# Splitting weight pieces two per pair, with five places for raw pieces

## The chip, the cores and the metric

The kernel runs on one core of one Trainium2 chip. The metric is the device time of one execution in microseconds; the median of three runs of the kernel before is 1560.1 us (1558.79 to 1561.29). The engines are named PE (TensorE, the matrix engine), DVE (VectorE), ACT (ScalarE), POOL (GpSimd) and SP (SyncE, which here only issues DMA transfers).

## The reference: what is computed

Two layers over 2048 tokens of width 512. Each layer first gates its input with a bidirectional recurrence along time (`cond`), then applies a mixture of experts and adds the result to its input:

```
x = x + ffn0(cond0(x, f, f))   # 8 experts of inner width 256, top 2, one shared expert, RMS norm
x = x + ffn1(cond1(x, f, f))   # 32 experts of inner width 352, top 6, two shared halves
```

In the second layer, for each token t and each of its six experts e with softmax weight g(t, e):

```
h = silu(x[t] @ w1[e]) * (x[t] @ w3[e])
y[t] += g(t, e) * (h @ w2[e])
y[t] += (silu(x[t] @ sw1) * (x[t] @ sw3)) @ sw2     # shared, for every token
```

All matrices are float32. The weights of the 32 routed experts are 32 x 128 x 4352 numbers of 4 bytes as the kernel packs them, and each is read once.

## The kernel before: how the work is laid out and ordered

**Float32 by two halves.** A float32 operand is multiplied as a sum of two float16 values, high and low. A product takes three matmuls: high by high, high by low, low by high. So every weight piece that arrives raw from memory has to be split: ACT scales and rounds it into the high half `Whi` (function `w_hi_`, L1289), then DVE makes the low half as the raw value minus the high one (`w_lo`, L1719 for the wide part and L1722 for a strip of 64 columns). Some earlier pieces are split by POOL instead.

**Pieces.** The weights are cut into 163 pieces (`PIECES`): 0 to 26 belong to the first layer, 27 to 34 to the shared halves of the second, 35 on to its routed experts, four pieces of 128 x 1088 numbers (544 KB) for each expert. Pieces 51 to 54 are expert 4, 55 to 58 expert 5, and so on to piece 162, the last of expert 31. Ten pieces (`AHEAD`) land in unused parts of the weight tiles. All others pass through a ring of two places, `ST`: SP's `w_load` (L1021) of a piece waits until the low half of the piece two before it in the ring is made. `spare` (L824) says which block must be done before a piece's final place in `Whi` and `Wlo` may be overwritten: six experts have places at a time.

**Order.** Every engine runs its part of one list of stages, produced by the generator `stages` (L136). Engines are in order: an instruction that waits holds back all that stand behind it on its engine. `loads(n, upto)` puts up to n loads into the list, of pieces below `upto`, as long as the ring of two has room; `splits(n)` puts in n splits; `weights(n, upto)` does n times loads, one split, loads.

**The second layer.** First the shared halves (32 blocks) are computed while the rows are gated, stored and given their logits. Then the table of places is made: `r_place` and `hot` on DVE with `hot_pe` on PE, and `table1`, which gives the list of rows for each block of 128. POOL gathers the rows of a block by that table (L1118). The gather needs the gate weights `Wd` stored in memory by SP (`r_wts`, L1018).

The routed part is 128 blocks, four to an expert, done as 64 pairs. A pair has three tiles `f_gu` (PE L1988 and L1994: gate and up products, transposed, with both blocks of the pair side by side), for each of which ACT takes a tanh, DVE multiplies, and `f_split` splits the result (ACT L1343, DVE L1766). Then come two `down` (PE L2059), one for each block; ACT evicts the result (L1365) and POOL adds it to the output rows by an indirect accumulating DMA (L1136). A pair's `down` stand in the list within the next pair: the first after the next pair's first tile, the second after its third. Rows of coming blocks are transposed for the tiles either on PE with a copy on ACT (`turn`, L1917 and L1300) or by a DMA transpose issued by SP (`x_turn`, L1010): `by_pe` chooses PE for the first twelve blocks and for every second one afterwards, so pairs 0 to 4 turn both blocks of the next pair on PE, later ones one.

`pair_weights(p)` (L569) is called twice in each pair: after the first `down`, and after the third tile, before the second `down`. It calls `weights`: nothing in pairs 0 and 1, two pieces in each call in pairs 2 to 5, one in each call from pair 6 on. Its limit `ready` keeps loads and splits to pieces whose places are free by then; it rises by four pieces every second pair.

The tiles `FD` and `FN` (L676) belong to the recurrence and to the sum of the first layer's results, `XR` (L686) to the gating of rows. None of them is used in the routed part. `FH`, `FU` and `FS`, which the routed part does use, are in `RT`.

Of the kernel before, what the change touches and what calls it, by code (L numbers as in the profile page):

```python
# [5 lines left out]
P = 128  # L6
T = 2048
D = 512
NT = T // P
ROWS = T + 512  # L10
CAP = 512
F32 = mybir.dt.float32
# [89 lines left out]
def pieces():  # L102
    out = []
    for e in (8, 0, 1, 2, 3, 4, 5, 6, 7):
        for c in range(3):
            out.append((0, e, c * 1024, 1024, e * 3072 + c * 1024, "pool" if 3 <= len(out) < 15 or len(out) % 2 else "dve"))
    for m, e in enumerate([32, 33] + list(range(32))):
        for c in range(4):
            pool = 2 <= m < SLOTS1
            out.append((1, e, c * 1088, 1088, place1(e) + c * (1152 if e < 32 else 1088), "pool" if pool else "dve"))  # L110
    return out


PIECES = pieces()
# [5 lines left out]
AHEAD = (17, 18, 19, 20, 27, 28, 29, 30, 33, 34)  # L120
AHEAD_AT = (18432, 21504, 0, 24576, 3072)
RING = [k for k in range(len(PIECES)) if k not in AHEAD]


def low_count(k):
# [10 lines left out]
def stages():  # L136

    done = dict(load=0, hi=0, lo=0)

    def loads(n, upto):  # L140

        for _ in range(n):
            k = RING[done["load"]] if done["load"] < len(RING) else len(PIECES)
            if k < upto and done["load"] < sum(j < done["lo"] for j in RING) + 2:
                yield "w_load", k
                done["load"] += 1

    def splits(n, low=True):
        for _ in range(n):
            if done["hi"] in AHEAD or done["hi"] in RING[:done["load"]]:  # L150
                yield "w_hi", done["hi"]
                done["hi"] += 1
                if low:
                    yield from low_half()
# [6 lines left out]
    def weights(n, upto):  # L161
        for _ in range(n):
            yield from loads(2, upto)
            yield from splits(1)
            yield from loads(2, upto)
# [309 lines left out]
    for s in range(18):  # L475
        f = NT + s
# [53 lines left out]
        yield from loads(2, 51)  # L530

    yield "r_place", 3
    yield "r_wts", 7
    yield from shared(29, "gu_pe")
    yield from shared(28, "h_turn")
# [32 lines left out]

    def pair_weights(p):  # L569

        if p >= 2:
            ready = 63 + 4 * ((2 * p - 6) // 4) if p >= 3 else 59
            yield from weights(2 if p < 6 else 1, min(ready, len(PIECES)))

    def tile_in(t, what):

# [51 lines left out]
def build(nc, xtok, fT, cst, svec, cond, rout, gatew, W0, W1, Y1):  # L628
    with ExitStack() as ctx:
        ctx.enter_context(nc.allow_low_precision(reason="sums of at most 16 ones are exact in float16"))  # L630

        def sb(name, shape, dt=F32):
            return ctx.enter_context(nc.sbuf_tensor(name, shape, dt))

        def sem(name):
            return ctx.enter_context(nc.semaphore(name))
# [31 lines left out]
        Whi = sb("Whi", [P, 9 * 3072], F16)  # L668
        Wlo = sb("Wlo", [P, 9 * 3072], F16)
        ST = [sb(f"ST{i}", [P, 1088]) for i in range(2)]  # L670
# [2 lines left out]
        EK = sb("wkEK", [P, 512])  # L673
        EU = [sb(f"wkEU{i}", [P, 512]) for i in range(2)]
        EKV = sb("wkEKV", [P, 512])
        FD = [sb(f"wkFD{i}", [P, 512]) for i in range(2)]  # L676
        FN = [sb(f"wkFN{i}", [P, 512]) for i in range(2)]
        RT = [sb(f"RT{i}", [P, 4, 512]) for i in range(2)]
        HT32 = sb("HT32", [P, 512])
        cnd = HT32[:, :].rearrange("p (b k) -> p b k", b=4)  # L680
# [2 lines left out]
        XSp = [XSall[:, i, :, :] for i in range(4)]  # L683
        XG = [sb(f"XG{i}", [P, D + 32]) for i in range(3)]
        zero, squares = XG[0], XG[2]
        XR = [sb(f"XR{i}", [P, 512])[:, :] for i in range(4)] + [XG[i][:, 0:512] for i in range(2)]  # L686

        X1 = [K[0], K[1], EU[0], EU[1], EK, EKV]
        PK = [[FD[0], FN[0]], [FD[1], FN[1]]]
        WSL = sb("WSL", [P, 8])  # L690
# [39 lines left out]
        gaps = [Wlo[:, e * 4608:e * 4608 + 4608].rearrange("p (r n) -> p r n", r=4)[:, :, 1024:1152] for e in range(4)]  # L730
        AB = [gaps[0:2], gaps[2:4], [W[:, 27136:27648].rearrange("p (r n) -> p r n", r=4) for W in (Whi, Wlo)]]
        idt = OT[:, 0:128]
        XG1 = [XG[i][:, :] for i in range(3)] + [OH[:, 0:D + 32]]


# [12 lines left out]
        d_pick = [sem(f"d_pick{i}") for i in range(2)]  # L748
        d_first = sem("d_first")
        d_w = [sem(f"d_w{i}") for i in range(2)]  # L750
        d_ahead = [sem(f"d_ahead{i}") for i in range(len(AHEAD))]
        d_g = [sem(f"d_g{i}") for i in range(3)]
        d_g1 = [sem(f"d_g1{i}") for i in range(4)]
        d_t = [sem(f"d_t{i}") for i in range(4)]
# [15 lines left out]
        f_part, f_x1, f_tanh, f_gate, f_sq, f_var, f_pow, f_turned, f_ht, f_hi, f_lo, f_lgm, f_lg = (sem(n) for n in (  # L770
            "f_part", "f_x1", "f_tanh", "f_gate", "f_sq", "f_var", "f_pow", "f_turned", "f_ht", "f_hi", "f_lo", "f_lgm", "f_lg"))
# [28 lines left out]
        def low(k):  # L800
            who, count = low_count(k)
            return (w_lov if who == "dve" else w_lop), count
# [11 lines left out]
        def staged(k):  # L814

            l, e, c0, cw, at, who = PIECES[k]
            if k in AHEAD:
                m = AHEAD.index(k)
                to = AHEAD_AT[m // 2]
                return (Whi, Wlo)[m % 2][:, to:to + 2 * cw].bitcast(F32), d_ahead[m], 16  # L820
            m = RING.index(k)
            return ST[m % 2][:, 0:cw], d_w[m % 2], 16 * (m // 2 + 1)

        def spare(k):  # L824

# [22 lines left out]
        def place_of(z):  # L848
# [9 lines left out]
            if z < 71:  # L858
                return XG[2][:, 0:512].bitcast(F16)
            return XG1[(z - 71) % 4][:, 0:512].bitcast(F16)  # L860

# [77 lines left out]
        def _(eng):  # L939
# [35 lines left out]
            def x_load(f):  # L975
# [3 lines left out]
                if f == 4:  # L979
                    eng.wait_ge(d_zero, 16 * 12)  # L980
                S.dma_start(XR[f % 6], xtok[f * P:f * P + P, :]).then_inc(d_x[f % 6], 16)

# [38 lines left out]
            def w_load(k):  # L1021
                l, e, c0, cw, at, who = PIECES[k]
                if k not in AHEAD and k >= 2:
                    eng.wait_ge(*low(RING[RING.index(k) - 2]))
                if k in AHEAD and l == 1:


                    eng.wait_ge(b_down, R0 + {24576: 0, 0: NT, 3072: 2 * NT}[AHEAD_AT[AHEAD.index(k) // 2]])
                at, there, count = staged(k)
                S.dma_start(at, WD[l][e][:, c0:c0 + cw]).then_inc(there, 16)  # L1030
# [25 lines left out]
        def _(eng):  # L1056
# [7 lines left out]
            def k_num_(n):  # L1064
                eng.wait_ge(k_sn, n + 1)
                eng.wait_ge(k_euv, n + 1)
                if n + 1 < 32:

                    eng.wait_ge(k_min, n + 2)
                G.tensor_tensor(FN[n % 2][:, :], FN[n % 2][:, :], EU[n % 2][:, :], ALU.add).then_inc(k_num, 1)  # L1070

# [17 lines left out]
            def gather(n):  # L1089
# [18 lines left out]
                else:  # L1108
# [5 lines left out]
                    if j >= 4:  # L1114
                        x_read(eng, xslot(n - 4))
                        eng.wait_ge(b_wsl, j - 3)
                    to, there = XG1[j % 4], d_g1[j % 4]
                G.indirect_dma_start(  # L1118
# [42 lines left out]
        def _(eng):  # L1161
# [20 lines left out]
            def k_fwd(n):  # L1182
# [4 lines left out]
                eng.wait_ge(k_fd, n + 1)  # L1187
                A.activation(FD[n % 2][:, 0:511], FD[n % 2][:, 0:511], ACT.Copy, scale=gain).then_inc(k_gd, 1)
                eng.wait_ge(k_fn, n + 1)
                A.activation(FN[n % 2][:, 0:511], FN[n % 2][:, 0:511], ACT.Copy, scale=gain).then_inc(k_gn, 1)  # L1190

# [18 lines left out]
            def f_tanh_(f):  # L1210
                if f < NT:
                    eng.wait_ge(d_x[f % 6], 16 * (f // 6 + 1))
                    src = XR[f % 6]
                else:
# [5 lines left out]
                    if f % 6 in (4, 5):  # L1220
                        for z in (S1 - 3, S1 - 2):
                            x_there(eng, z)
                A.activation(XR[f % 6], src, ACT.Tanh, scale=0.5).then_inc(f_tanh, 1)

            def f_sq_(f):
                eng.wait_ge(f_gate, f + 1)
                if f >= 1:
                    eng.wait_ge(f_sq, f)
                A.activation(squares[:, 0:512], XR[f % 6], ACT.Square, accum_out=sm[:, f, 0:1]).then_inc(f_sq, 1)

            def f_hi_(f):
# [10 lines left out]
                if z > S1:  # L1242

                    eng.wait_ge(d_row[(f - 1) % 6], 16 * rows_stored(f - 1))
                    x_there(eng, z - 1)
                A.activation(place_of(z)[:, 0:512], XR[f % 6], ACT.Copy,
                             scale=sm[:, f, 2:3] if l == 0 else XS).then_inc(f_hi, 1)
# [127 lines left out]
        def _(eng):  # L1375
# [49 lines left out]
            def k_fwd(n):  # L1425
                f = FN[n % 2]
                eng.wait_ge(k_min, n + 1)
                V.tensor_tensor_scan(FD[n % 2][:, :], decay(n), EK[:, :], 0.0, ALU.mult, ALU.add).then_inc(k_fd, 1)  # L1428
                eng.wait_ge(k_ekv, n + 1)
# [4 lines left out]
            def k_bwd(n):  # L1434

                f = FN[n % 2]
                dc = decay(n)[:, 0:511]
                eng.wait_ge(k_gd, n + 1)
                V.tensor_tensor_scan(FD[n % 2][:, 510::-1], dc, FD[n % 2][:, 510::-1], FD[n % 2][:, 511:512], ALU.mult,  # L1439
                                     ALU.add).then_inc(k_sd, 1)  # L1440
# [4 lines left out]
            def k_den_(n):  # L1445
                u = EU[n % 2]
                eng.wait_ge(k_eu, n + 1)
                eng.wait_ge(k_sd, n + 1)
                V.scalar_tensor_tensor(out=FD[n % 2][:, :], in0=u[:, :], scalar=E30, in1=FD[n % 2][:, :], op0=ALU.min,  # L1449
                                       op1=ALU.add).then_inc(k_den, 1)  # L1450
# [4 lines left out]
            def k_rec_(n):  # L1455
                eng.wait_ge(k_den, n + 1)
                V.reciprocal(FD[n % 2][:, :], FD[n % 2][:, :]).then_inc(k_rec, 1)  # L1457

            def k_out_(n):
                f = FN[n % 2]  # L1460
                eng.wait_ge(k_num, n + 1)
# [5 lines left out]
            def gate(f):  # L1467
# [4 lines left out]
                if l == 1 and i >= 8:  # L1472
                    eng.wait_ge(d_back[i - 8], 16)
                x = XR[f % 6]
                V.scalar_tensor_tensor(out=x, in0=x, scalar=1.0, in1=RT[b % 2][:, q, :],
# [250 lines left out]
            def weight(n):  # L1726
# [4 lines left out]
                if j >= 8:  # L1731
                    eng.wait_ge(b_outa, NB0 + j - 7)
                V.tensor_copy(WSL[:, n % 8:n % 8 + 1], XG1[j % 4][:, D + e:D + e + 1]).then_inc(b_wsl, 1)

# [396 lines left out]
```

## Time and profile before

| | |
|---|---|
| median of three runs | 1560.1 us (1558.79 to 1561.29) |
| the profiled execution, its own time | 1559.94 us |
| its span in the trace | 1558.1 us |
| PE busy | 1313.3 us, 84% of the span |
| DVE busy | 1084.5 us, 70% |
| ACT busy | 780.9 us, 50% |
| POOL busy | 616.6 us, 40% |
| mean granted PE clock | 0.951 of full |

The span is the time from the first to the last instruction in the profile. "Busy" counts computing instructions. The granted clock is the share of full speed that TensorE was given. A line number such as L1766 is a line of the kernel before. "ST<-W" is a transfer of a raw weight piece into the ring. In the timelines, the bracket behind an instruction gives how long its engine stood idle before it, and what ended the idle time.

### The profile page before, as it was taken

To read this page: it belongs to the slowest core of one execution; us is meant where nothing else is said; L and a number is where in the kernel's file an instruction comes from. 1 tells how busy PE (TensorE), PEld (TensorE's weight loads), DVE (VectorE), ACT (ScalarE), POOL (GpSimd) and SP (SyncE) were. 2 spreads that over 40 slices of the span, in tenths; PEclk is the share of its full clock that TensorE was granted. 3 is DMA by queue.
4 is the path that set the end of the run, shared out by engine and by line. 5 is a ranking of instruction groups with operands and counts; after the bars stand their busy time and mean duration, and the time that the engine had idled before them with its cause. 6 is when DMAs were issued, how large, how long until landed. Compare 5 with 4: busy or idle time off the path is not lost.

```text
span 1558.1 us, 26165 instructions
## 1 busy us (share of the span) xinstructions
PE 1313.3 (84%) x9124; PEld 883.9 (57%) x9124; DVE 1084.5 (70%) x2186; ACT 780.9 (50%) x1451; POOL 616.6 (40%) x478
## 2 busy tenths in 40 slices
PE   0046565599999599999897999999999999999997
PEld 0023352244444366566565677777777777777775
DVE  8999988979898668888655555665565656556332
ACT  4466654645554453441255455555555555555333
POOL 2343443444342343330133444444444444444442
PEclk9988766899999799999999999999999999999999
DMA  3557556677896686541258899989998899899664
GB/s 104 170 162 200 145 117 135 133 194 179 225 247 156 178 225 182 160 132 50 94 147 196 171 212 214 206 202 216 200 214 214 194 222 200 207 226 190 116 117 59
DMA packets 224191, 269.28 MB, mean 173 GB/s; under 512 B 148608, under 2 KB 148736, under 8 KB 223936
## 3 DMA queue, kind: packets, MB, share of 16 engines
q1 hardware_dynamic: 187408, 175.58, 44.5%
q0 software_dynamic: 36656, 92.03, 27.8%
q8 instruction: 76, 1.25, 0.3%
q14 instruction: 51, 0.42, 0.1%
HBM read 167.87 MB, written 70.32 MB: 153 GB/s over the span
## 4 chain that ended last, share of the span: by engine, by line
PE 66%; DVE 22%; issue 5%; DMA 3%; ACT 3%; POOL 0%; SPq 0%; POOLq 0%; ACTq 0%; DVEq 0%
PE psO L2059 21%; PE psG L1988 20%; PE psG L1956 10%; DVE wkFD L1457 5%; PE psH L1988 5%; PE psG L1994 3%; DMA ST<-W 3%; DVE wkFD L1439 2%; PE psX L1917 2%; DVE wkFN L1432 2%; DVE wkFD L1428 2%; DVE Wlo L1719 1%; DVE wkFN L1464 1%; DVE wkFD L1449 1%; ACT Whi L1289 1%
## 5 line engine op out<-in xcount | busy, mean ns | idle before, releaser
L1136 POOL DMA_INDIRECT out<-OB,posb x128 | 221.2, 1728 | 393.1 <-ACT OB L1365 288.9
L1988 PE MATMUL psG<-XSp,Whi 128*128 128x256 f16 x2048 | 342.7, 273 | 2.5 <-ACT XSp L1300 2.5
L1988 PE MATMUL psG<-XSp,Wlo 128*128 128x256 f16 x1024 | 279.6, 273 | 0.0
L1956 PE MATMUL psG<-Whi,XSp 128*128 128x352 f16 (+2 forms) x952 | 258.6, 362 | 9.7 <-issue 8.4
L2059 PE MATMUL psO<-Whi,RT 128*128 128x512 f16 x768 | 253.4, 385 | 14.9 <-DVE RT L1766 14.9
L1719 DVE SCALAR_TENSOR_TENSOR Wlo<-ST,Whi 128x1024 f16<-128x1024 f32 (+1 forms) x116 | 142.2, 1226 | 160.0 <-ACT Whi L1289 154.8
L1988 PEld LDWEIGHTS psG<-XSp,Whi 128*128 128x128 f16 x2048 | 200.4, 98 | 47.9 <-ACT XSp L1300 2.8
L1747 DVE SCALAR_TENSOR_TENSOR RT<-RT,psG 128x256 f32<-128x256 f32 (+1 forms) x154 | 64.6, 419 | 134.5 <-ACT RT L1335 130.7
L1956 PEld LDWEIGHTS psG<-Whi,XSp 128*128 128x128 f16 x952 | 97.6, 103 | 102.0 <-issue 32.5
L1956 PE MATMUL psG<-Wlo,XSp 128*128 128x352 f16 (+2 forms) x476 | 151.6, 363 | 0.0
L1365 ACT ACTIVATE OB<-psO,WSL 128x512 f32<-128x512 f32 x128 | 87.3, 682 | 123.3 <-PE psO L2059 118.4
L2059 PE MATMUL psO<-Wlo,RT 128*128 128x512 f16 x384 | 147.7, 385 | 0.0
L2059 PE MATMUL psO<-Whi,HS 128*128 128x512 f16 (+1 forms) x412 | 140.2, 389 | 0.5 <-DVE OB L1795 0.5
L1289 ACT ACTIVATE Whi<-ST 128x1088 f16<-128x1088 f32 (+1 forms) x116 | 128.1, 1106 | 16.7 <-DMA ST<-W 15.6
L2059 PEld LDWEIGHTS psO<-Whi,RT 128*128 128x128 f16 x768 | 75.9, 99 | 104.2 <-DVE RT L1766 22.5
L1118 POOL DMA_INDIRECT XG<-xrows,posb x96 | 96.3, 1003 | 97.2 <-DVE posb L1649 54.8
L1335 ACT ACTIVATE RT<-psG 128x256 f32<-128x256 f32 (+1 forms) x154 | 58.8, 382 | 113.1 <-PE psG L1988 87.7
L1070 POOL TENSOR_TENSOR wkFN<-wkFN,wkEU 128x512 f32<-128x512 f32 x32 | 40.5, 1266 | 186.7 <-DVE wkEK L1419 175.6
L1457 DVE RECIPROCAL wkFD<-wkFD 128x512 f32<-128x512 f32 x32 | 107.0, 3345 | 0.0
L1988 PEld LDWEIGHTS psG<-XSp,Wlo 128*128 128x128 f16 x1024 | 100.3, 98 | 11.7
L1821 PE MATMUL psX<-C,wkFN 128*128 128x128 f32 x64 | 16.2, 401 | 100.7 <-DVE wkFN L1464 100.7
L1083 POOL TENSOR_TENSOR Wlo<-ST,Whi 128x1024 f16<-128x1024 f32 x33 | 70.2, 2128 | 68.5 <-ACT Whi L1293 68.5
(254 smaller groups left out, 2564.5 us busy)
## 6 DMA issues: line engine op xcount, KB each, us to landing
ST<-W SPq DMA_DIRECT2D x130, 544.0 KB
ST<-W SPq DMA_DIRECT2D x23, 512.0 KB
slots<-OB SPq DMA_DIRECT2D x39, 256.0 KB
wkK<-fT SPq DMA_DIRECT2D x32, 256.0 KB
xrows<-XG SPq DMA_DIRECT2D x20, 256.0 KB, 3.3
y0rows<-x SPq DMA_DIRECT2D x8, 512.0 KB, 5.3
y0rows<-OB POOLq DMA_DIRECT2D x16, 256.0 KB
out<-OB SPq DMA_DIRECT2D x16, 256.0 KB
```

Source lines behind the costliest of these rows:

```text
L1083: op = G.tensor_tensor(Wlo[:, at:at + w], st[:, 0:w], Whi[:, at:at + w], ALU.subtract)
L1118: G.indirect_dma_start(out=to, out_offset=None, in_=X[l][:, :], in_offset=bass.IndirectOffsetOnAxis(ap=idx[l][:, j:j + 1], axis=0)).then_i ...
L1136: G.indirect_dma_start(out=Y1[:, :], out_offset=bass.IndirectOffsetOnAxis(ap=idx[1][:, j:j + 1], axis=0), in_=OB[o % 4][:, :], in_offset=N ...
L1289: op = A.activation(st if who == "pool" else hi, st, ACT.Copy, scale=WS)
L1335: A.activation(FH[p % 2][0:rows, c, :], f_psum(t)[0:rows, 0:256], ACT.Tanh, scale=0.5 * UN).then_inc(b_ftanh, 1)
L1365: A.activation(OB[o % 4][:, :], psO[bank(o)][:, :], ACT.Copy, scale=scale).then_inc(b_outa, 1)
L1457: V.reciprocal(FD[n % 2][:, :], FD[n % 2][:, :]).then_inc(k_rec, 1)
L1719: op = V.scalar_tensor_tensor(out=Wlo[:, at:at + w], in0=st[:, 0:w], scalar=WS, in1=Whi[:, at:at + w], op0=ALU.mult, op1=ALU.subtract)
L1747: V.scalar_tensor_tensor(out=H[0:rows, :], in0=H[0:rows, :], scalar=1.0, in1=ps[0:rows, 0:256], op0=ALU.add, op1=ALU.mult).then_inc(b_fsil, 1)
L1956: op = M.matmul(o, hx[:, x, q * P:q * P + P], w(half_, off + c, nn), start=first, stop=last)
L1988: op = M.matmul(sums(half_ * 256), W[:, to:to + P], x(which, q), start=(q == 0 and which == 0 and W is Whi), stop=(q == 3 and W is Wlo))
L2059: op = M.matmul(psO[bank(o)][:, :], h(x, q), w(half_, off0 + q * 512), start=(q == 0 and x == 0 and half_ is Whi and first), stop=(q == NK ...
```

## The change

In `pair_weights`, pairs 1 on split one piece in each call (two per pair), instead of two in each call in pairs 2 to 5 and one from pair 6 on. The number of places for raw pieces is five from piece 51 on: the two of `ST`, and three in a new tensor `FX`, which also holds what were the tiles FD, FN and XR 0 to 3. A load waits for the low half of the piece five before it; the loads into the three new places wait, the first time, until the rows that used that memory are turned and split (`f_x1`, `f_turned`, `f_lo`). The limit `ready` holds for splits only. The first five loads (pieces 51 to 55) stand in the list behind the last `r_place` and ahead of the last `r_wts`, of the last `hot`s and of `table1`. The semaphores of the AHEAD pieces are used again for the five places, counted on from their first use.

```diff
--- before.py
+++ after.py
@@ -120,6 +120,7 @@
 AHEAD = (17, 18, 19, 20, 27, 28, 29, 30, 33, 34)
 AHEAD_AT = (18432, 21504, 0, 24576, 3072)
 RING = [k for k in range(len(PIECES)) if k not in AHEAD]
+WIDE = RING.index(51)
 
 
 def low_count(k):
@@ -141,7 +142,7 @@
 
         for _ in range(n):
             k = RING[done["load"]] if done["load"] < len(RING) else len(PIECES)
-            if k < upto and done["load"] < sum(j < done["lo"] for j in RING) + 2:
+            if k < upto and done["load"] < sum(j < done["lo"] for j in RING) + (2 if k < 51 else 5):
                 yield "w_load", k
                 done["load"] += 1
 
@@ -530,6 +531,7 @@
         yield from loads(2, 51)
 
     yield "r_place", 3
+    yield from loads(5, 56)
     yield "r_wts", 7
     yield from shared(29, "gu_pe")
     yield from shared(28, "h_turn")
@@ -568,9 +570,11 @@
 
     def pair_weights(p):
 
-        if p >= 2:
+        if p >= 1:
             ready = 63 + 4 * ((2 * p - 6) // 4) if p >= 3 else 59
-            yield from weights(2 if p < 6 else 1, min(ready, len(PIECES)))
+            if done["hi"] < min(ready, len(PIECES)):
+                yield from splits(1)
+            yield from loads(5, len(PIECES))
 
     def tile_in(t, what):
 
@@ -673,8 +677,9 @@
         EK = sb("wkEK", [P, 512])
         EU = [sb(f"wkEU{i}", [P, 512]) for i in range(2)]
         EKV = sb("wkEKV", [P, 512])
-        FD = [sb(f"wkFD{i}", [P, 512]) for i in range(2)]
-        FN = [sb(f"wkFN{i}", [P, 512]) for i in range(2)]
+        FX = sb("FX", [P, 8 * 512])
+        FD = [FX[:, i * 512:i * 512 + 512] for i in range(2)]
+        FN = [FX[:, i * 512 + 1024:i * 512 + 1536] for i in range(2)]
         RT = [sb(f"RT{i}", [P, 4, 512]) for i in range(2)]
         HT32 = sb("HT32", [P, 512])
         cnd = HT32[:, :].rearrange("p (b k) -> p b k", b=4)
@@ -683,7 +688,7 @@
         XSp = [XSall[:, i, :, :] for i in range(4)]
         XG = [sb(f"XG{i}", [P, D + 32]) for i in range(3)]
         zero, squares = XG[0], XG[2]
-        XR = [sb(f"XR{i}", [P, 512])[:, :] for i in range(4)] + [XG[i][:, 0:512] for i in range(2)]
+        XR = [FX[:, i * 512 + 2048:i * 512 + 2560] for i in range(4)] + [XG[i][:, 0:512] for i in range(2)]
 
         X1 = [K[0], K[1], EU[0], EU[1], EK, EKV]
         PK = [[FD[0], FN[0]], [FD[1], FN[1]]]
@@ -730,6 +735,7 @@
         gaps = [Wlo[:, e * 4608:e * 4608 + 4608].rearrange("p (r n) -> p r n", r=4)[:, :, 1024:1152] for e in range(4)]
         AB = [gaps[0:2], gaps[2:4], [W[:, 27136:27648].rearrange("p (r n) -> p r n", r=4) for W in (Whi, Wlo)]]
         idt = OT[:, 0:128]
+        STW = [ST[WIDE % 2], ST[1 - WIDE % 2]] + [FX[:, i * 1088:i * 1088 + 1088] for i in range(3)]
         XG1 = [XG[i][:, :] for i in range(3)] + [OH[:, 0:D + 32]]
 
 
@@ -748,7 +754,7 @@
         d_pick = [sem(f"d_pick{i}") for i in range(2)]
         d_first = sem("d_first")
         d_w = [sem(f"d_w{i}") for i in range(2)]
-        d_ahead = [sem(f"d_ahead{i}") for i in range(len(AHEAD))]
+        d_staged = [sem(f"d_staged{i}") for i in range(len(AHEAD))]
         d_g = [sem(f"d_g{i}") for i in range(3)]
         d_g1 = [sem(f"d_g1{i}") for i in range(4)]
         d_t = [sem(f"d_t{i}") for i in range(4)]
@@ -817,9 +823,12 @@
             if k in AHEAD:
                 m = AHEAD.index(k)
                 to = AHEAD_AT[m // 2]
-                return (Whi, Wlo)[m % 2][:, to:to + 2 * cw].bitcast(F32), d_ahead[m], 16
+                return (Whi, Wlo)[m % 2][:, to:to + 2 * cw].bitcast(F32), d_staged[m], 16
             m = RING.index(k)
-            return ST[m % 2][:, 0:cw], d_w[m % 2], 16 * (m // 2 + 1)
+            if m < WIDE:
+                return ST[m % 2][:, 0:cw], d_w[m % 2], 16 * (m // 2 + 1)
+            i = (m - WIDE) % 5
+            return STW[i][:, 0:cw], d_staged[i], 16 * ((m - WIDE) // 5 + 2)
 
         def spare(k):
 
@@ -1021,7 +1030,16 @@
             def w_load(k):
                 l, e, c0, cw, at, who = PIECES[k]
                 if k not in AHEAD and k >= 2:
-                    eng.wait_ge(*low(RING[RING.index(k) - 2]))
+                    m = RING.index(k)
+                    if m < WIDE + 2:
+                        eng.wait_ge(*low(RING[m - 2]))
+                    elif m < WIDE + 5:
+
+                        eng.wait_ge(f_x1, NT)
+                        eng.wait_ge(f_turned, 2 * NT)
+                        eng.wait_ge(f_lo, 2 * NT)
+                    else:
+                        eng.wait_ge(*low(RING[m - 5]))
                 if k in AHEAD and l == 1:
```

## Rows read from the trace of the kernel before

**Rows 1.** The page, part 2: busy tenths of PE and DMA engines, 40 slices.

```profile
PE   0046565599999599999897999999999999999997
...
DMA  3557556677896686541258899989998899899664
```

**Rows 2.** Windows: length, busy of PE, PEld, DVE, ACT, POOL, clock, DMA share, GB/s.

```profile
789.79:869.22 79.43, 66.99 (x497) 47.09 (x495) 43.13 (x98) 42.04 (x69) 27.96 (x20) 0.91 0.77 177
869.22:1438.90 569.68, 568.77 (x4514) 421.43 (x4513) 337.86 (x815) 315.40 (x576) 264.21 (x192) 1.00 0.92 208
```

**Rows 3.** Timeline of PE, 800 to 870: start, length, instruction, idle before, releaser.

```profile
806.92 0.60 PE L2059 MATMUL psO<-Whi,RT 128*128 128x512 f16 x1 [2.30 <-DVE RT L1766]
...
824.95 0.61 PE L2059 MATMUL psO<-Whi,RT 128*128 128x512 f16 x1 [3.97 <-DVE RT L1766]
...
841.94 0.39 PE L2059 MATMUL psO<-Whi,RT 128*128 128x512 f16 x1 [1.72 <-DVE RT L1766]
...
858.32 0.61 PE L2059 MATMUL psO<-Whi,RT 128*128 128x512 f16 x1 [4.45 <-DVE RT L1766]
```

**Rows 4.** Chain of waits, 798 to 805: start, length, what.

```profile
798.77 5.11 DMA ST<-W
...
803.90 1.12 ACT Whi L1289
```

**Rows 5.** Waits of POOL and SP, 795 to 905: total us, times, longest.

```profile
POOL out L1136 <- DMA out<-OB,posb: 12.3, 4, 3.7
...
SPq L1030 <- DVE Whi L1722: 81.1, 16, 31.2
```

**Rows 6.** Chain of waits, stamps in the routed part.

```profile
789.79 2.62 PE psG L1988 x24
...
866.83 0.45 PE psX L1917 x8
...
869.22 2.62 PE psG L1988 x24
...
1000.49 2.62 PE psH L1988 x24
...
1057.79 1.94 PE psO L2059 x9
1059.73 2.62 PE psH L1988 x24
1062.35 2.03 PE psO L2059 x9
```

**Rows 7.** Window around the second of the four waits.

```profile
824.00:832.00 8.00, 7.05 (x30) 3.85 (x31) 3.01 (x9) 2.88 (x4) 5.38 (x4) 0.57 0.65 172
```

**Rows 8.** Chain of waits at pair 15, and PE's timeline behind it.

```profile
965.69 6.34 DMA ST<-W
...
979.34 0.39 PE L2059 MATMUL psO<-Whi,RT 128*128 128x512 f16 x1 [0.91 <-DVE RT L1766]
```

**Rows 9.** DMA issues, one line, a window, timelines of SP and POOL.

```profile
Whi<-W SPq DMA_DIRECT2D x3, 544.0 KB, 5.8
...
L1457 DVE RECIPROCAL wkFD<-wkFD x32: 3332/3346/3347, 17.0 to 496.9; 128x512 f32<-128x512 f32 x32
...
760.00:772.00 12.00, 9.51 (x75) 6.67 (x76) 2.85 (x9) 2.52 (x4) 4.25 (x5) 1.00 0.83 275
...
742.04 0.38 SPq L1018 DMA_DIRECT2D xrows<-Wd  x1
...
758.26 0.96 POOL L1118 DMA_INDIRECT XG<-xrows,posb  x1 [54.81 <-DVE posb L1649]
```

**Rows 10.** L1010, the DMA transposes: one issue, all landings, PE's wait.

```profile
1002.97 8.44 SPq L1010 DMA_TRANSPOSE XSp<-XG  x2
...
DMA to landing us min/median/max: 2.8/4.5/9.3
...
PEld psG L1988 <- DMA XSp<-XG: 0.3, 1, 0.3
```

## The prediction, made before the changed kernel was run

> **What bounds the kernel now.** I read the page's slices first [rows 1]: behind slice 14 PE falls below nine tenths only in slice 20 (8), the passage into the routed part, whose pairs run from 767 us on, and in slice 22 (7), 818 to 857 us, inside it. The table by stretches says how much that is: from 869.22 to 1438.90 PE is busy 568.77 of 569.68 us at a clock of 1.00, while 789.79 to 869.22 has 66.99 busy of 79.43 at 0.91 [rows 2]. So the routed part is bound by TensorE, and what a change of the weight supply can give back is what PE loses to waiting, plus what it then loses to the lower clock.
>
> PE's own timeline names the waits [rows 3]: 2.30, 3.97, 1.72 and 4.45 us, 12.44 in all, each before the first matmul of a `down` (L2059) and each released by DVE L1766, the second half of `f_split`. That step doesn't need the weights just split. The chain of waits shows why it is late [rows 4]: a transfer "DMA ST<-W" of 5.11 us, and right behind its landing ACT L1289, then DVE L1719. ACT and DVE work in order, so a split whose raw piece has not landed stands ahead of the eviction, the cast and the subtraction that `down` waits for. With four splits per pair and two places a load can start only once the piece two before it is split, so from the third piece on each split waits for a whole transfer; SP waited 81.1 us in 16 such waits [rows 5].
>
> The pairs are read from stamps in the chain [rows 6]. Pair 2 begins at 789.79, pair 7 at 869.22. With two splits per pair, 1000.49 and 1059.73 are the same tile five pairs apart: 59.24 us, 11.85 a pair. In it the first `down` of a pair takes 2.03 for its nine matmuls, the second 1.94: 0.09 late behind the split at the end of the pair before.
>
> **The change part by part.** *Two splits per pair from pair 1 on.* The same pieces are split by the same instructions (ACT 1.12 us [rows 4]), but one in each of the two calls of `pair_weights`, as in the steady part. An ideal for pairs 2 to 6 follows from rows. Pairs 0 to 4 turn both blocks of the next pair on PE; one such turn is 0.45 us (L1917) [rows 6]. Pairs 2, 3 and 4 are then 11.85 + 0.45 = 12.30, pairs 5 and 6 11.85: 36.90 + 23.70 = 60.60 us. They take 79.43. The difference is 18.83: 12.44 of idle PE and 6.39 of slower matmuls. The granted clock was 0.57 between 824 and 832, around the wait that ended at 824.95 [rows 7], and 1.00 in the stretch behind 869 without such waits: the lower of the two levels, 1.2 GHz for 2.4, comes after PE has stood still. Without the waits both go.
> The Trainium skill ("TensorE: Matmul & The Clock Gate", Part 1) has the same shape: the slow clock is the resting state of the array. By it the 6.39 us have no cause of their own and go with the waits. Another cause of the dips, were there one, would leave the 6.39 us in: 1546.9 by the sum below, and that is part of the first rival.
> Pair 1 gets two splits that it did not have. They cost it between nothing and their whole length on ACT, 2 by 1.12; I take what they cost a steady pair, 0.1, since the two places in the order are the same. The queue is now behind that of before (piece 63 next at pair 7, was 67), so the last piece is split two pairs later, in pair 56: twice 0.1 more. Expert 4 (pieces 51 to 54) is ready in pair 2 and needed in pair 8, each later one likewise six pairs ahead, some 70 us.
>
> *Five places.* In steady flow each split releases one load, as before, but the load is for the piece five on, so it has some 2 pairs (24 us) before its split, against 5.8 us median for a transfer of that size [rows 9]. Before, the limit `ready` made loads come in bursts: at pair 15 one asked for at 965.69 took 6.34 us, and PE lost 0.91 behind it [rows 8]. That is the only idle PE between 869 and 1439 [rows 2], and it goes: -0.91, or 0 if something else takes its place.
> The places are FD, FN and XR made into one tensor. Moving tiles costs nothing that rows show: the reciprocals on the two FD tiles take 3332 to 3347 ns [rows 9]. 15 ns by 32 is 0.5 us either way; I take 0 and keep this end.
>
> *Five loads ahead of the table.* SP issues them before the Wd store at 742.04, and their waits (row tiles turned and split) are fulfilled by then. Issuing costs SP 5 by 0.38 = 1.9 us (the Wd store's own 0.38 taken for each) [rows 9]. SP waits there for DVE to make Wd, which hides it; without that cover it is 1.9. The transfers are 5 by 544 KB, 2.79 MB. At the 275 GB/s that 760 to 772 shows this is 10 us, one after the other at 5.8 us it is 29. Started near 732, ten us ahead of the store, they have landed between 742 and 761. Behind them comes the Wd store, which the first gather needs at 758.26 [rows 9]. So the cost lies between 0 and some 761 + 2 - 758.3 = 4.7 us (2 for the store itself, an estimate from a size an eighth of a piece's). The DMA engines are busy one to two tenths in slices 19 and 20 [rows 1], so I take 0. Below nothing: two loads no longer meet the first gathers, and PE is idle 12.00 - 9.51 = 2.5 us in 760 to 772; that much at most comes back, I take 0, since the gathers were issued before those loads.
> The Trainium skill ("DMA: Bandwidth & Descriptors", Queues, rings and completion order) says that each DMA engine works through the descriptors of one issuer's row in ring order. By it the Wd store has to stand behind all five loads; by the first rate it still lands at about 745, and the sum stays; by the second it costs the 4.7. The same rule makes the third rival below possible.
>
> **Sum**: 1559.94 (profiled execution, span 1558.1) - 18.83 - 0.91 + 0.1 + 0.2 = 1540.5. The median of the runs, 1560.1, is 0.2 from it: 1540.6 us as forecast of the median. Everything downstream is shifted only: the last matmuls and the last scatters come at the same distance.
>
> **Rivals.**
> 1. *A new wait takes the place.* Pairs 1 to 4 have one more turn on PE (0.45 us) with its copy on ACT than the steady pairs, and scatters and gathers start there. If a wait of 1 us per pair stayed in pairs 1 to 6 and held the clock down as before, half of it again, 6 by 1.5 = 9 us come back: 1549.6. For: `f_split` already is 0.09 late in every steady pair [rows 6], so there is no slack. Against: the added copy comes before the tile that ACT waits for anyway. Chance 0.08.
> 2. *The Wd store is held up* by the five loads: +4.7, 1545.3. Against: the idle DMA engines. Chance 0.03.
> 3. *Slower: the transposes miss their pair.* The block transposes (L1010) stand on SP behind the load that waits for the second split. Before, that was so in every other pair, because `ready` kept loads out of the rest; now it is so in every pair from 5 on. In such a pair the transpose is issued 2.5 us after the pair's start (1002.97 against 1000.49), and the next pair starts 9.4 us later (1000.49 + 11.85) [rows 6, 10]. Landings were 2.8 to 9.3 us, median 4.5, and PE waited for one once, 0.3 us [rows 10]. If the newly exposed 24 or so pairs landed 1 us past that, 24 us go: 1564.5. It decides from 0.8 us mean overshoot on. Against: some 25 pairs had this order already, with one wait of 0.3 us seen [rows 10]. Chance 0.04.
> 4. *It does not do what it says:* the early pairs stay late for another reason, for example the scatters, for which POOL waits 12.3 us between 795 and 905 [rows 5]. Near 1560. Against: these waits are POOL's, and ACT's eviction is not shown waiting for them. Chance 0.03.
>
> **How the numbers follow.** The forecast has 0.82. Its own range is 1537.6 (2.5 at the start and 0.5 of tiles come back) to 1544 (pair 1 costs 2.2, the 0.9 stays). The range given is 1537.5 to 1548: with the main case and parts of rivals 1 and 2, some 0.88. A measurement of this kernel tells about 0.2% (3 us) from no change. Faster by over 0.2%: 0.82 + 0.08 + 0.03 = 0.93; same 0.03 (rival 4); slower 0.04 (rival 3).
>
> **What would show it.** Right: PE busy all through 790 to 850 at clock 1.00; no "DMA ST<-W" in the chain after 765; pair 7's first tile at about 850.5; splits at two per pair from about 783 on, the last two pairs later in count, five pairs still at 59.24; five loads between 732 and 742; first gather still at 758. Wrong: an idle entry at L2059 in the early pairs (rival 1), the first gather later than 758.3 with "xrows<-Wd" landing late (2), PEld waits on "DMA XSp<-XG" spread over the routed part and five pairs above 59.3 (3), or pair 7 again at 869 (4).

## The result, and the profile after

The changed kernel takes 1550.5 us (median of 7 runs, 1549.59 to 1564.81); the kernel before 1562.24 (7 runs, the three of its own table among them, 1558.79 to 1564.6). The ratio is 0.9939, 95% interval 0.9912 to 0.9965: faster by 0.6%, half of the forecast 1.25%, and 2.5 us above the upper end of the range. The spread is new: 15 us between its runs, for 6 before. All ratios here and below leave out runs more than 1.5% above the fastest of their kernel, which is one run, of the kernel with two places. The profiled execution is the slowest of the seven, 1564.81 us, with a span of 1563.0; so its losses stand for the bad end of that spread.

The slices, PE and DMA, against [rows 1]: slice 22 now holds a 9, but slices 27 (1016 to 1055 us) and 29 (1094 to 1133 us), which held a 9, have an 8.

```profile
PE   0046675599999599999899999989899999999997
...
DMA  3557546678995686543269999999999989999664
```

Windows of the changed kernel, with the columns of [rows 2]. The first runs from the first tile of pair 2 to the end of the last `down` in pair 6, the second is the stretch of [rows 2].

```profile
789.71:850.23 60.52, 60.52 (x494) 44.99 (x492) 35.38 (x86) 35.65 (x64) 27.43 (x20) 1.00 0.80 170
869.22:1438.90 569.68, 552.72 (x4346) 408.06 (x4344) 326.37 (x783) 303.62 (x554) 254.78 (x187) 0.99 0.98 201
```

The early pairs are what the sum said: 60.52 us, PE busy in all of them, clock at 1.00 (forecast 60.60; before, 79.43). The stretch behind, which had 0.91 us of idle PE, now has 569.68 - 552.72 = 16.96. The waits of the changed kernel between 852 and 1440 (total us, times, longest) say for what:

```profile
POOL out L1154 <- DMA out<-OB,posb: 120.4, 22, 10.4
PEld psG L2006 <- DMA XSp<-XG: 17.1, 9, 4.0
PE psG L2006 <- DMA XSp<-XG: 13.0, 7, 3.5
PEld psH L2006 <- DMA XSp<-XG: 7.3, 3, 3.6
PE psH L2006 <- DMA XSp<-XG: 5.7, 2, 3.1
```

On the weight-load side PE waited 17.1 + 7.3 = 24.4 us in 12 places for DMA transposes; before, 0.3 in one [rows 10]. On the matmul side PE stood still for 18.7 us. The forecast's sum in terms of the span was 1538.7; 1563.0 - 1538.7 = 24.3. The 5.6 us between 18.7 and 24.3 fit slower matmuls: in the second stretch one takes 552.72 / 4346 = 127.2 ns for 568.77 / 4514 = 126.0 before, some 5 us in all, at a granted clock of 0.99 for 1.00. So in this execution the transposes account for the whole difference. The chain of waits shows one of them, at pair 22:

```profile
1031.18 1.02 ACT Whi L1307
...
1033.36 0.23 DVE Whi L1740
...
1033.61 0.33 SPq L1048
...
1034.04 12.44 DMA XSp<-XG
...
1046.53 2.79 PE psH L2006 x24
```

Second split of pair 21 on ACT, its end on DVE, then SP's load (L1048, the old L1030), which waited for it, then the transpose (L1019, the old L1010) behind that load: 12.44 us to landing, and the first tile of the next pair starts with it. No wait for a raw piece (ST<-W, FX<-W) is left in the routed part.

### The profile page after: what moved, and what is told of

It reads as the page before. It is cut to its first block, busy times and chain, and to the rows that moved or that the text cites. A ratio compares the mean times of both kernels' runs of the same rounds, so it can differ in the third digit from the quotient of the medians.

```text
span 1563.0 us, 26168 instructions
## 1 busy us (share of the span) xinstructions
PE 1316.7 (84%) x9124; PEld 884.0 (57%) x9124; DVE 1085.6 (69%) x2186; ACT 779.8 (50%) x1451; POOL 616.0 (39%) x478
## 3 DMA queue, kind: packets, MB, share of 16 engines
q8 instruction: 76, 1.25, 0.3%
## 4 chain that ended last, share of the span: by engine, by line
PE 61%; DVE 22%; DMA 7%; issue 6%; ACT 3%; SPq 0%; POOL 0%; POOLq 0%; ACTq 0%; DVEq 0%
PE psG L2006 19%; PE psO L2077 18%; PE psG L1974 9%; DMA XSp<-XG 6%; DVE FX L1475 5%; PE psH L2006 5%; PE psG L2012 3%; DVE FX L1457 2%; DVE FX L1450 2%; DVE FX L1446 2%; PE psX L1935 2%; DVE FX L1482 1%; DVE FX L1467 1%; DVE FX L1460 1%; DVE H L1793 1%
## 5 line engine op out<-in xcount | busy, mean ns | idle before, releaser
L2077 PE MATMUL psO<-Whi,RT 128*128 128x512 f16 x768 | 249.6, 380 | 1.5 <-DVE RT L1784 1.5
L2006 PEld LDWEIGHTS psG<-XSp,Whi 128*128 128x128 f16 x2048 | 200.6, 98 | 63.0 <-DMA XSp<-XG 17.1
L1737 DVE SCALAR_TENSOR_TENSOR Wlo<-FX,Whi 128x1024 f16<-128x1024 f32 x66 | 80.9, 1226 | 88.6 <-ACT Whi L1307 83.5
L1088 POOL TENSOR_TENSOR FX<-FX,wkEU 128x512 f32<-128x512 f32 x32 | 40.5, 1266 | 185.3 <-DVE wkEK L1437 174.1
L1475 DVE RECIPROCAL FX<-FX 128x512 f32<-128x512 f32 x32 | 107.1, 3346 | 0.0
L1737 DVE SCALAR_TENSOR_TENSOR Wlo<-ST,Whi 128x1024 f16<-128x1024 f32 (+1 forms) x50 | 61.4, 1228 | 61.9 <-ACT Whi L1307 61.8
L1839 PE MATMUL psX<-C,FX 128*128 128x128 f32 x64 | 16.3, 404 | 99.2 <-DVE FX L1482 99.2
```

The lines of the kernel that those rows point to most:

```text
L1737: op = V.scalar_tensor_tensor(out=Wlo[:, at:at + w], in0=st[:, 0:w], scalar=WS, in1=Whi[:, at:at + w], op0=ALU.mult, op1=ALU.subtract)
L2006: op = M.matmul(sums(half_ * 256), W[:, to:to + P], x(which, q), start=(q == 0 and which == 0 and W is Whi), stop=(q == 3 and W is Wlo))
L2077: op = M.matmul(psO[bank(o)][:, :], h(x, q), w(half_, off0 + q * 512), start=(q == 0 and x == 0 and half_ is Whi and first), stop=(q == NK ...
```

## The experiments

Two theories. **A, the order on SP:** in the changed kernel every transpose stands behind a load that waits for the second split. It is issued late, its data stand behind 544 KB in the same queue, and its packets then run among the scatters'. **B, the traffic:** five places and denser loads slow the transposes whatever the order.

**The changed kernel again.** 

> The changed kernel once more, beside the others. In its first trace pairs 2 to 6 took what was forecast, but TensorE waited 24.4 us (weight-load side) for DMA transposes, in 12 places, while its time went from 1549.6 to 1564.8 us between runs. Both theories: about 1550 us median, some 10 us under before, with a spread of several us, and waits on 'DMA XSp<-XG' of 8 to 25 us in the profile.

Measured: 1553.92 us (7 runs, 1543.31 to 1558.15), before 1562.11 (18 runs); ratio 0.9931 (0.9904 to 0.9958). Its profile has waits of 14.1 + 2.1 us on transposes in 7 places. The loss is there again, in other pairs and of another size.

**Loads held by `ready`.**

```diff
-            yield from loads(5, len(PIECES))
+            yield from loads(5, min(ready, len(PIECES)))
```

> The changed kernel with the limit `ready` put back on the loads only: five places, two splits per pair and the five loads ahead stay. The second call of every second pair then issues no load, so the transposes of every second pair go out at once, as before the change. Theory A (a transpose that stands behind a load, which itself waits for the second split, is issued some 2.5 us late in every pair, and meets the scatters and gathers): the waits on transposes fall to under 3 us, the spread goes, 1541 to 1544 us. Rival B (the transposes are slow because of what five places let onto the DMA engines, whatever the order): no better than the changed kernel, about 1550.

Measured: 1541.04 us (1539.45 to 1544.54), ratio 0.987 (0.9849 to 0.9891). No wait on a transpose is left. SP's timeline shows both kinds of pair. The transpose at 1061.38 goes out with no waiting load right ahead of it; the one at 1076.97 stands behind three loads (from 1064.70 on), the last of them waiting for a split.

```profile
1058.60 0.33 SPq L1048 DMA_DIRECT2D ST<-W  x1
1061.38 1.24 SPq L1019 DMA_TRANSPOSE XSp<-XG  x1
1064.70 12.18 SPq L1048 DMA_DIRECT2D FX<-W  x3
1076.97 1.24 SPq L1019 DMA_TRANSPOSE XSp<-XG  x1
```

Five places, the early loads and the number of bytes are as in the changed kernel. What differs is when loads go out, and with it that only every second transpose stands behind one. So five places alone are not the cause. That the loads now come in bursts is a difference too; the kernel after the next one has no bursts.

**Two places.** The kernel before, with one split per call from pair 1 on:

```diff
-        if p >= 2:
+        if p >= 1:
             ready = 63 + 4 * ((2 * p - 6) // 4) if p >= 3 else 59
-            yield from weights(2 if p < 6 else 1, min(ready, len(PIECES)))
+            yield from loads(2, len(PIECES))
+            if done["hi"] < min(ready, len(PIECES)):
+                yield from splits(1)
+            yield from loads(2, len(PIECES))
```

> The kernel before with one part of the change alone: one split per call from pair 1 on, and loads not held by `ready`; two places, the old memory, no loads ahead of the table. A load follows each split, as in the changed kernel. Theory A: the early waits go (the load has about a pair's time), the transposes stand behind a load in every pair, so like the changed kernel, 1547 to 1556. Rival B: without the five places the transposes land in time, 1541 to 1544. If the early gain needs the five loads ahead, a wait for ST<-W shows in pair 1 to 3 instead.

Measured: 1557.65 us (12 runs, 1547.84 to 1571.29), ratio 0.9965 (0.994 to 0.9991). The median (1557.01 without the highest run) is above the range given by A; with that spread I don't read more from it than that the loss is there without the five places. Together with the loads held by `ready`, B falls. Waits and chain of its profile:

```profile
PEld psG L1991 <- DMA XSp<-XG: 11.4, 6, 4.1
...
839.18 12.96 DMA XSp<-XG
```

No wait on ST<-W stands in it: with one split per call, a load has about a pair's time, and two places are enough.

**The load behind the transpose.** The changed kernel, the second call without its load, and the load after the next pair's `x_turn`:

```diff
         yield from turn(n + 2, False)
+        if p >= 2:
+            yield from loads(5, len(PIECES))
...
-        yield from pair_weights(p)
+        yield from pair_weights(p, False)
```

> The changed kernel with the load of the second call moved in the list behind the next pair's x_turn, nothing else: no transpose stands behind a load that waits for the second split, in any pair. Theory A: every transpose is issued about when the pair starts and lands within 4 us; no waits on transposes, 1540 to 1542 us. Rival B: the same traffic, so waits as before, about 1550.

Measured: 1541.81 us (1539.8 to 1545.54), ratio 0.9873 (0.9851 to 0.9896), no wait on a transpose. A transpose of SP's timeline, and the first tile of the pair from the chain: the transpose for the pair after goes out 2.3 us before this pair starts.

```profile
1072.96 1.24 SPq L1022 DMA_TRANSPOSE XSp<-XG  x1
...
1075.28 2.62 PE psG L2009 x24
```

The loads are not held by `ready` here, and nothing but their place behind the transpose differs from the changed kernel. So the order is the cause. What in it? A late issue, a load ahead, or both together? Three kernels part them.

**Late, but nothing ahead.** The order above, and each transpose also waits for the second split:

```diff
             def x_turn(z):
+                if z >= 71:
+                    eng.wait_ge(*low(halved[-1]))
```

`halved[-1]` is the last split that stands in the list before the transpose.

> The order of e3 (load behind the transpose), but each transpose of the routed part also waits for the second split of the pair before, so it is issued as late as in the changed kernel (about 2.2 us after the pair's start) with no load ahead of it. If the lateness alone is what makes the transposes miss: waits on them as in the changed kernel, 1549 to 1556. If the load ahead in the queue is needed: 1541 to 1543.

Measured: 1543.26 us (1540.56 to 1545.47), ratio 0.9887 (0.9867 to 0.9906), no wait on a transpose though it is issued 2.06 us into the pair:

```profile
1077.99 1.42 SPq L1025 DMA_TRANSPOSE XSp<-XG  x1
...
1075.93 2.62 PE psG L2013 x24
```

**Early, but behind a load.** The load is held until the transpose may go, and issued right ahead of it:

```diff
+            def w_load_at(kz):
+                k, z = kz
+                gathered(eng, z)
+                x_free(eng, ring_before(z))
+                w_load(k)
```

In the list `w_load_at` stands right ahead of `x_turn(z)`.

> Five places, but the second load of a pair is held until the next transpose may go and is issued directly ahead of it, without waiting for the last split. The transpose is early (about 0.4 us before the pair's start) and stands behind a load's 544 KB. If standing behind the load is enough to miss: waits as in the changed kernel, 1549 to 1556. If lateness is needed too: packets of the transposes run some 3 us after the issue, end before the pair's scatters, 1541 to 1543.

Measured: 1539.69 us (1539.38 to 1541.41), ratio 0.9865 (0.9846 to 0.9884), no wait. A load and its transpose, and the start of the pair, 1.16 us later (1.9 in the middle case):

```profile
1061.36 0.33 SPq L1056 DMA_DIRECT2D ST<-W  x1
1061.78 1.24 SPq L1027 DMA_TRANSPOSE XSp<-XG  x1
...
1062.94 2.62 PE psG L2020 x24
```

**At the eviction, nothing ahead.**

```diff
             def x_turn(z):
+                if z >= 71:
+                    eng.wait_ge(b_outa, routed_of(z - 4))
```

> The order of e3, but each transpose of the routed part waits for ACT's eviction of the pair's first block, the same event that releases POOL's scatter, some 5.4 us after the pair's start; no load stands ahead of it. The next pair starts 6.4 us later. If what counts is that the transpose's packets run together with a scatter's: landings well above 6.4 us, waits in many pairs, above 1560. If a load ahead is needed: a landing takes the 4.5 us of the others, few waits, 1541 to 1546.

Measured: 1541.53 us (4 runs, 1539.41 to 1542.38), ratio 0.9876 (0.9838 to 0.9914). Issued 5.41 us into the pair, later than in any other kernel, the transposes still land in time, but for two waits of 1.1 us in all:

```profile
1067.78 1.24 SPq L1025 DMA_TRANSPOSE XSp<-XG  x1
...
1062.37 2.62 PE psG L2012 x24
...
PEld psH L2012 <- DMA XSp<-XG: 0.6, 1, 0.6
PEld psG L2012 <- DMA XSp<-XG: 0.5, 1, 0.5
```

Neither lateness alone nor a load ahead alone costs anything. My expectation here assumed that a transpose released with the scatter meets it. It doesn't: its packets come after the scatter's (packet records below).

**Small scatters.** The changed kernel, but POOL's routed scatters write 16 rows of each block's 128; the other rows of the routed result are left out.

```diff
-  ...(ap=idx[1][:, j:j + 1], axis=0), in_=OB[o % 4][:, :], ...
+  ...(ap=idx[1][0:16, j:j + 1], axis=0), in_=OB[o % 4][0:16, :], ...
```

> The changed kernel, whose routed scatters write 16 of 128 rows of each block and leave the others out (the loads, the transposes and their order stay). If the transposes are slow because their small packets run among those of the scatters (and the gathers that these push back): waits on transposes under 1 us in all, 1538 to 1541. If the weight loads are what slows them: waits as in the changed kernel, about 1550.

Measured: 1535.81 us (4 runs, 1535.41 to 1537.04), ratio 0.9836 (0.9814 to 0.9858). Loads and transposes stand as in the changed kernel, load first, 0.42 us apart, and no transpose makes PE wait; POOL's own wait for scatters between 780 and 1540 us is down from 132.2 us in the changed kernel (first line) to 36.6:

```profile
POOL out L1154 <- DMA out<-OB,posb: 132.2, 27, 10.4
...
POOL out L1154 <- DMA out<-OB,posb: 36.6, 24, 2.9
...
1065.02 0.33 SPq L1048 DMA_DIRECT2D FX<-W  x1
1065.44 1.24 SPq L1019 DMA_TRANSPOSE XSp<-XG  x1
```

So the late order does harm only with full scatters beside it (and the gathers that they push). The time is 2.2 us under the range expected and 3.9 under the best of the others; that fits the shorter last scatters, but was not taken apart.

**What the packets show.** The trace keeps the record of every single DMA packet: a transpose is 1024 packets of 256 bytes, a scatter's packets are of 2048 bytes, a gather's and a load's of 4352. The table has the medians of some 50 transposes of each trace, issued between 835 and 1440 us. "Issue" is against the start of the pair, "first" and "last" are the first and the last packet against the issue, "ns" is the mean time of its packets, "scatter" and "gather" are how many packets of these fell between the first and the last, and "slow" counts transposes whose last packet came more than 7.5 us after the issue. Even and odd pairs stand apart where they differ ("only two parts" is the last kernel below).

```
kernel                        issue   first   last    ns   scatter  gather   slow
before, even pairs            +2.5    +2.5    +6.2    36   96       6        3
before, odd pairs             -1.0    +1.2    +2.7    21   2        0        0
changed                       +2.5    +2.6    +6.2    38   108      10       18
two places                    +2.5    +2.7    +6.1    32   108      12       9
loads by ready, even          +2.5    +2.5    +5.9    29   97       4        2
loads by ready, odd           -1.2    +2.1    +3.8    27   1        0        0
load behind transpose, even   -2.3    +1.5    +5.0    29   100      0        0
load behind transpose, odd    -2.3    +2.1    +4.2    30   2        0        0
only two parts, even          -2.3    +1.5    +4.9    31   112      0        0
only two parts, odd           -2.3    +2.1    +3.8    25   2        0        0
late, nothing ahead           +2.1    +1.2    +2.6    21   3        0        0
early, behind a load, even    -1.9    +3.1    +5.8    22   112      0        0
early, behind a load, odd     -1.9    +2.6    +5.4    36   0        0        0
at the eviction               +5.4    +2.0    +4.3    22   0        60       0
changed, 16-row scatters      +2.5    +2.7    +4.4    22   12       26       0
```

A load directly ahead moves the first packet from +1.2 to between +2.5 and +3.1. Alone that is harmless, as 2.1 us of late issue are. Together they put the transposes where a scatter and the gathers behind it run: the 18 slow ones of the changed kernel met 124 scatter and 46 gather packets in the middle case, and there a 256-byte packet takes 60 ns and not 21. At the eviction the transposes are later still and have slipped past the scatter: none met.

Neither kind of packet is enough alone. In the three kernels "load behind transpose", "only two parts" and "early, behind a load", 51 transposes met 80 or more scatter packets and under 10 gather packets; the latest last packet among them is at +7.1. (Of such transposes issued late behind a load, 2 of 11 in the kernel before and 1 of 9 in the changed one are slow, at +7.9 at most.) At the eviction and with 16-row scatters, 89 met 20 or more gather packets and under 20 scatter packets; there the latest is at +5.9. In the changed kernel 25 met 80 or more scatter and 10 or more gather packets, and 16 of them are slow. A transpose that is slow also has more time to meet others, so the counts alone don't say what comes first. The small scatters show that the scatter's packets are needed; no run takes the gathers away.

The Trainium skill ("DMA: Bandwidth & Descriptors", Queues, rings and completion order) has both halves: one issuer's descriptors are consumed in ring order on each engine, and an engine takes turns between the rows that have work, packet by packet. The shift by 1.3 to 1.9 us behind a load agrees with the first. The second agrees in kind; in size it is not enough by itself, since 124 scatter packets at 0.25 us, their mean in the changed kernel, over 16 engines are 1.9 us (worked out from this case's packet records), and the last packet of the 18 slow transposes comes at +9.8, 3.6 us later than the middle one, which met 108.

**Only two parts.** The kernel before, one split per call from pair 1, and the second load behind the transpose. Two places, nothing ahead of the table, the old memory:

```diff
-    def pair_weights(p):
+    def pair_weights(p, load=True):
-        if p >= 2:
+        if p >= 1:
-            yield from weights(2 if p < 6 else 1, min(ready, len(PIECES)))
+            if p == 1 and load:
+                yield from loads(2, len(PIECES))
+            if done["hi"] < min(ready, len(PIECES)):
+                yield from splits(1)
+            if load:
+                yield from loads(2, len(PIECES))
...
         yield from turn(n + 2, False)
+        if p >= 2:
+            yield from loads(2, len(PIECES))
...
-        yield from pair_weights(p)
+        yield from pair_weights(p, False)
```

> The kernel before with one split per call from pair 1 on, and the second load of a pair behind the next pair's x_turn; two places, no loads ahead of the table, the old memory. If the five places and the early loads are worth nothing here, as the traces of e2 suggest (no wait on ST<-W in it): 1541 to 1543, like e3. If the places matter once the loads are one transpose later: waits on ST<-W and 1545 or more.

Measured: 1540.57 us (1539.04 to 1542.53), ratio 0.9868 (0.9849 to 0.9887). First tile of pair 2 and of pair 7 in its chain, 60.59 us apart:

```profile
788.54 2.62 PE psG L1995 x24
...
849.13 2.62 PE psG L1995 x24
```

This is as good as the best with five places (1539.69, intervals overlap) and beats both the kernel before and the changed one.

## Why the prediction was wrong

**Two splits per pair: right, to 0.1 us.** Pairs 2 to 6 take 60.52 us against 60.60 forecast, at full clock, so the 6.39 us of slower matmuls went with the 12.44 of waits. Six kernels with this step, the full scatters and at most 2 of some 50 transposes over 7.5 us measure 1539.7 to 1543.3, the forecast being 1540.6.

**Five places: the step that failed.** The sum gave them -0.91 for the load burst at pair 15, and that wait is gone. But the other effect of letting loads run past `ready`, a load that waits for a split ahead of every transpose, was put among the rivals with 0.04, and it is what happened: 24.4 us in the profiled execution, about 10 in the median. The reasons given against it were two, and both were weak:

- "Landings were 2.8 to 9.3 us" [rows 10]. The changed kernel's answer of the same kind reads 3.1/4.4/6.7, while its chain shows transposes of 10.4 to 13.7 us. That line speaks only for the transposes whose landing the view can tell, and none of these is in the routed part: asked for 780 to 1540 us alone, it gives no landing in either kernel. The chain and the packets do. In the kernel before, the last packet of a transpose behind a load came at +6.2 us in the middle case and at +8.6 at most, of the 9.4 us that the prediction counted; the median of 4.5 promised 4.9 us of room where there were 3.2.
- "Some 25 pairs had this order already", with one wait of 0.3 us. True, but in the kernel before each such pair was followed by one without a load in front. Slack that exists in every second pair is not slack in a row. Of the 12 waits in the changed kernel, 8 are for transposes issued in even pairs, and 7 of these stood behind such a load before, too. Their surroundings had changed, not their place in the list. Of the 4 in odd pairs, the newly exposed ones (6.3 of the 24.4 us), 3 come right behind a wait: those issued in pairs 7, 27 and 35 follow those of 6, 26 and 34. With `ready` back on the loads, every second pair is free again and no wait is left.

The size in the rival was right for the slowest execution (24 us, 1564.5 against 1564.81 measured) and wrong for the middle one. Its point of decision was a mean of 0.8 us over the 24 newly exposed pairs. The profiled execution has 24.4 / 24 = 1.0, and is indeed slower than the median of before (1562.24); the median execution has some 10 / 24 = 0.4, and the change stays faster. That the 24 us agree is luck: they were worked out as 1 us in each newly exposed pair, and three quarters of the measured waits are in the other pairs.

**Five early loads: right, and worth nothing.** SP issued them at 732.20 to 734.8, and the Wd store and the first gather came when they had before (742.04 and 758.26 in [rows 9]). Timelines of SP and POOL in the changed kernel:

```profile
732.20 0.92 SPq L1048 DMA_DIRECT2D ST<-W  x2
733.23 1.55 SPq L1048 DMA_DIRECT2D FX<-W  x3
741.95 0.38 SPq L1027 DMA_DIRECT2D xrows<-Wd  x1
...
758.18 0.96 POOL L1136 DMA_INDIRECT XG<-xrows,posb  x1 [54.38 <-DVE posb L1667]
```

The bound of 2.5 us below nothing came to 9.59 - 9.51 = 0.08 us of PE:

```profile
760.00:772.00 12.00, 9.59 (x76) 6.74 (x77) 2.85 (x8) 2.44 (x4) 4.16 (x5) 1.00 0.60 182
```

The kernel with two places and no early loads is as fast as those with both, so neither carries any of the gain.

**The other rivals.** No wait at `down` took the place of the old ones (rival 1), Wd was not held up (rival 2), and the early pairs did not stay late (rival 4).

**What stays open.** Why the loss varies by 15 us between executions of one program, and why it comes in clusters of pairs (9 of the 12 waits of the first trace are for transposes issued in pairs 20 to 48, 7 of them in pairs 20 to 35). POOL's waits for its own scatters between 852 and 1440 us rose to 120.4 us from what they were in the kernel before:

```profile
POOL out L1136 <- DMA out<-OB,posb: 70.3, 22, 4.6
```

So a slow transpose may delay the scatter that meets the next one; that is argued, and no run isolates it. How much of a slow transpose is due to the scatter, how much to the gathers and the loads beside it, is open too.

## What to carry to other kernels

Where a load that waits for something is put into a queue, read what stands behind it: SP had idle time and free places, and still the load made a transpose late that it had nothing to do with. A limit that seems only to guard memory (`ready`) can also be what keeps a queue clear; ask what its removal lets through before taking it off. And count the parts of a change apart: here the pacing of the splits carried all the gain, provided that no waiting load stands ahead of every transpose, and the new places and the early loads carried none. A median over cases of two kinds can hide both: in the kernel before, transposes ended at +6.2 and at +2.7 us by turns.

## What was not expected of the hardware

A DMA transpose of 256-byte packets is cheap alone: 21 ns a packet, the last packet 2.6 us after the issue with nothing ahead. Beside a scatter's packets without gathers (100 to 112 met) a packet took 22 to 31 ns, beside gathers' without a scatter's (60 met) 22 ns. In the 18 slow cases, late behind a load and among both, a packet took 60 ns and the last one came at +9.8 in the middle case. So later can be better: issued 5.4 us into the pair, past the scatter, it lands sooner after its issue (+4.3) than at 2.5 us behind a load (+6.2).
